# Cross-attention on one core: probability transposes issued two pairs further ahead, into four PSUM banks, in blocks of sixteen and eight

## What is computed

```python
q = _split_heads(hidden_states @ w_q, HEADS)
k = _split_heads(text @ w_k, HEADS)
v = _split_heads(text @ w_v, HEADS)
out_text = _sdpa(q, k, v)
...
k_ip = _split_heads(ip_h @ w_k_ip, HEADS)
v_ip = _split_heads(ip_h @ w_v_ip, HEADS)
out_ip = _merge_heads(_sdpa(q, k_ip, v_ip, mask=mask_ip))
out = out_text + IP_SCALE * out_ip
out = out @ w_out + b_out
out = out + residual
```

## Time and profile before

| what | value |
|---|---|
| median of 3 runs | 904.91 us (904.73 to 905.33) |
| the profiled execution's own time | 905.81 us |
| its span, first to last instruction | 904.0 us |
| PE busy | 882.5 us, 98% of the span |
| DVE, ACT, POOL busy | 726.6, 603.5, 540.0 us |
| mean granted TensorE clock | 0.992 of full speed |
| from group to group (start of scores to start of scores) | 50.4 to 50.5 us |

### The profile page before, as it was taken

One profiled execution on the slowest core, in us unless ns is written; L12 is line 12 of the kernel. 1 busy time (PEld: TensorE's weight loads), 2 busy tenths in 40 slices (PEclk: granted clock), 3 DMA queues, 4 the chain that ended last, 5 costly groups with the idle time before them and its releaser, 6 DMA issues.

```text
span 904.0 us, 13890 instructions
## 1 busy us (share of the span) xinstructions
PE 882.5 (98%) x4685; PEld 753.8 (83%) x4685; DVE 726.6 (80%) x1006; ACT 603.5 (67%) x986; POOL 540.0 (60%) x431
## 2 busy tenths in 40 slices
PE   7999999999999999999999999999999999999968
PEld 6889888888888888888888888888888888888846
DVE  6959579797888879797888879697888879797772
ACT  7556385876768485866767585867767584857550
POOL 5349669293755649293846648393847657392731
PEclk9999999999999999999999999999999999999978
DMA  9743322103030303003030303012030303010101
GB/s 318 271 162 117 96 69 86 44 1 131 1 124 1 131 0 102 21 13 118 0 123 0 131 0 122 2 33 98 0 123 0 131 0 116 0 59 1 47 12 59
DMA packets 34059, 64.63 MB, mean 71 GB/s; under 512 B 4464, under 2 KB 6512, under 8 KB 33904
## 3 DMA queue, kind: packets, MB, share of 16 engines
q1 hardware_dynamic: 33888, 62.97, 20.6%
q10 hardware_dynamic: 144, 1.31, 0.3%
HBM read 40.34 MB, written 23.59 MB: 71 GB/s over the span
## 4 chain that ended last, share of the span: by engine, by line
PE 82%; DVE 3%; ACT 1%; POOL 1%; issue 0%; DVEq 0%
PE bank L95 23%; PE bank L97 23%; PE bank L96 22%; PE bank L995 7%; PE bank L1004 4%; PE bank L1005 4%; DVE o_raw L905 1%; DVE pT_lo L898 1%; ACT oT_hi L820 0%; ACT pv_part L816 0%; POOL prob L185 0%; DVE total L226 0%; POOL prob L179 0%; DVE res L912 0%; ACT pT_hi L811 0%
## 5 line engine op out<-in xcount | busy, mean ns | idle before, releaser
L765 POOL TENSOR_TENSOR oT_lo<-o_raw,oT_hi 128x512 fp32r<-128x512 f32 x80 | 103.2, 1290 | 241.5 <-ACT oT_hi L820 241.5
L179 POOL TENSOR_TENSOR prob<-prob,top 128x1120 f32<-128x1120 f32 x126 | 178.8, 1448 | 0.0
L185 POOL TENSOR_TENSOR prob<-prob,inv 128x1120 f32<-128x1120 f32 x126 | 173.9, 1412 | 5.1 <-DVE inv L228 5.1
L95 PE MATMUL bank<-xT_hi,wq_hi 128*128 128x512 f32 x400 | 163.3, 408 | 0.0
L95 PE MATMUL bank<-oT_hi,wo_hi 128*128 128x512 f32 x400 | 156.7, 392 | 0.4 <-DVE res L912 0.4
L97 PE MATMUL bank<-xT_hi,wq_lo 128*128 128x512 f32 x400 | 156.8, 392 | 0.0
L96 PE MATMUL bank<-oT_lo,wo_hi 128*128 128x512 f32 x400 | 156.5, 391 | 0.0
L97 PE MATMUL bank<-oT_hi,wo_lo 128*128 128x512 f32 x400 | 156.5, 391 | 0.0
L96 PE MATMUL bank<-xT_lo,wq_hi 128*128 128x512 f32 x400 | 155.8, 389 | 0.0
L905 DVE TENSOR_TENSOR o_raw<-bank,pv_part 64x512 f32<-64x512 f32 x160 | 110.1, 688 | 47.2 <-ACT pv_part L816 44.8
L215 ACT ACTIVATE prob<-prob 128x1280 f32<-128x1280 f32 x64 | 81.6, 1277 | 78.6 <-POOL prob L179 78.5
(11 more groups left out here) (110 smaller groups left out, 1787.0 us busy)
## 6 DMA issues: line engine op xcount, KB each, us to landing
xin<-in_xT SPq DMA_DIRECT2D x16, 1280.0 KB, 6.8
outT<-res SPq DMA_DIRECT2D x80, 256.0 KB, 6.7
w_raw<-in_L_xattn_w_k SPq DMA_DIRECT2D x8, 320.0 KB, 5.6
w_raw<-in_L_xattn_w_k_ip SPq DMA_DIRECT2D x8, 320.0 KB, 5.7
w_raw<-in_L_xattn_w_v_ip SPq DMA_DIRECT2D x8, 320.0 KB, 3.1
w_raw<-in_L_xattn_w_v SPq DMA_DIRECT2D x8, 320.0 KB, 3.3
v_raw<-v_scratch SPq DMA_DIRECT2D x14, 140.0 KB
prob<-in_textT SPq DMA_DIRECT2D x8, 224.0 KB, 4.8
```

The source lines that it names most:

```text
L95: nc.tensor.matmul(dst, a_hi, b_hi, start=first, stop=False)
L179: ins = eng.tensor_tensor(s, s, top[:, t, n, :].unsqueeze(2).broadcast_to([P, HEADS, k1 - k0]), ALU.subtract)
L185: ins = eng.tensor_tensor(s, s, inv[:, t, n, :].unsqueeze(2).broadcast_to([P, HEADS, k1 - k0]), ALU.mult)
L765: nc.gpsimd.tensor_tensor(oT_lo[:, m, :], o_raw[:, m % 2, :], oT_hi[:, m, :].bitcast(F32), ALU.subtract).then_inc(oT_lo_done, 1)
```

## The change

- `t_bank` becomes banks 0 to 3 instead of 2 and 3, and pair p uses bank p % 4. The first four score units of a group now all wait for the last `pT_lo` of the group before.
- PE: the transposes of pairs 0 to 3 stand ahead of slot 0 (sixteen in a row). In slots 0, 1 and 2 the transposes of pairs 2s+4 and 2s+5 stand behind both pairs of the slot (eight in a row); slots 3 and 4 have none. Each waits for the `pT_lo` of pair p - 4.
- ACT and DVE: in each slot both `pT_part` now stand between the even and the odd move, or add. ACT's `pT_part(p)` gets a wait for `pv_ready` of pair p - 2, whose buffer of `pT_hi` it overwrites.

The buffers `pT_hi` and `pT_lo`, `v_bank`, and the waits of `pv_pair` stay as they are. No instruction that computes is added or removed.

```diff
-        s_bank, t_bank, v_bank = bank[0:4], bank[2:4], bank[4:6]
+        s_bank, t_bank, v_bank = bank[0:4], bank[0:4], bank[4:6]
...
         def score_unit(pe, g, n, b, new_batch):
-            if n < 2:
-                wait(pe, score_copied, UNITS * g)
-            elif n < 4:
+            if n < 4:
                 wait(pe, pT_lo_done, PAIRS * g)
...
                 def pT_part(g, p):
                     act.wait_ge(pT_ready, PAIRS * g + p + 1)
-                    nc.scalar.activation(pT_hi[:, p % 2, :], t_bank[p % 2][:], ACT.Copy).then_inc(pT_hi_done, 1)
+                    if p >= 2:
+                        act.wait_ge(pv_ready, PAIRS * g + p - 1)
+                    nc.scalar.activation(pT_hi[:, p % 2, :], t_bank[p % 4][:], ACT.Copy).then_inc(pT_hi_done, 1)
...
-                        for p in (2 * s, 2 * s + 1):
-                            move_pv(g, p)
-                            if p + 2 < PAIRS:
-                                pT_part(g, p + 2)
+                        move_pv(g, 2 * s)
+                        for p in (2 * s + 2, 2 * s + 3):
+                            if p < PAIRS:
+                                pT_part(g, p)
+                        move_pv(g, 2 * s + 1)
...
-                        for p in (2 * s, 2 * s + 1):
-                            add_pv(g, p)
-                            if p + 2 < PAIRS:
-                                pT_part(g, p + 2)
+                        add_pv(g, 2 * s)
+                        for p in (2 * s + 2, 2 * s + 3):
+                            if p < PAIRS:
+                                pT_part(g, p)
+                        add_pv(g, 2 * s + 1)
...
                 def p_transpose(g, p, shared):
-                    if p < 2:
+                    if p < 4:
                         pe.wait_ge(score_copied, UNITS * (g + 1))
                     else:
-                        pe.wait_ge(pT_lo_done, PAIRS * g + p - 1)
+                        pe.wait_ge(pT_lo_done, PAIRS * g + p - 3)
...
-                    p_transpose(g, 0, shared)
-                    p_transpose(g, 1, shared)
+                    for p in range(4):
+                        p_transpose(g, p, shared)
...
                         for p in (2 * s, 2 * s + 1):
                             pv_pair(g, p, b, new_batch)
-                            if p + 2 < PAIRS:
-                                p_transpose(g, p + 2, shared)
+                        for p in (2 * s + 4, 2 * s + 5):
+                            if p < PAIRS:
+                                p_transpose(g, p, shared)
```

More of the change, by code:

```diff
@@ L897, in pT_part @@
                     dve.wait_ge(pT_hi_done, PAIRS * g + p + 1)
-                    nc.vector.tensor_tensor(pT_lo[:, p % 2, :], t_bank[p % 2][:], pT_hi[:, p % 2, :].bitcast(F32), ALU.subtract).then_inc(pT_lo_done, 1)
+                    nc.vector.tensor_tensor(pT_lo[:, p % 2, :], t_bank[p % 4][:], pT_hi[:, p % 2, :].bitcast(F32), ALU.subtract).then_inc(pT_lo_done, 1)
                 def add_pv(g, p):
@@ L994, in p_transpose @@
                         src = prob[:, t * SW + p * P:t * SW + (p + 1) * P]
-                        ins = nc.tensor.transpose(t_bank[p % 2][:, t * P:(t + 1) * P], src, ident[:])
+                        ins = nc.tensor.transpose(t_bank[p % 4][:, t * P:(t + 1) * P], src, ident[:])
                     ins.then_inc(pT_ready, 1)
```

## The result

| | before | changed |
|---|---|---|
| median of 4 runs each | 904.84 us (904.73 to 905.33) | 939.79 us (938.98 to 939.95) |
| the profiled execution's own time, its span | 905.81, 904.0 us | 939.80, 938.0 us |
| start of scores to start of scores, groups 2 to 14 | 50.4 to 50.5 us | 52.4 to 52.7 us |
| first transpose to first score matmul, groups 2 to 14 | 19.35 to 19.51 us | 21.33 to 21.68 us |
| mean granted clock | 0.992 | 0.993 |

The changed kernel is slower by a factor of 1.0381 (95% interval 1.0367 to 1.0394), 35.0 us. The forecast was 937.2 us.

A forecast was written before the change was run, and what follows sets the result against it. PE, busy 98% of the span, bounds the kernel, with zero slack in ACT's and DVE's loop; 14 x 2.0 + 2.0 + 2.0 = +32 us gives 937.2 us on the median, range 926 to 952.

The forecast's parts named there:

- The even-move loop: ACT and DVE, one even move to the next: from 3.88 to 4.47 us with a q tile, 3.98 without.
- M0: End of slot 0's even move on ACT, forecast 5.05 us after the first transpose; M1 to M3 are slots 1 to 3.
- The waits on PE: PE in the values stage: pairs 5, 7, 8 and 9 wait 0.42, 0.15, 0.66 and 0.87 us.
- Group time: Each of the 16 groups, including 0 and 15, takes 2.0 us longer.
- Switches on PE: PE, fewer changes between transposes and matmuls: five joined runs save 0.02 to 0.03 us each, -0.1 us per group.
- pair 9's release: PE's last pair may start at M3 + 2.85 us, after slot 3's odd add on DVE; forecast 20.82 us.
- The far bound: PE, largest saving per switch between transposes and matmuls: 0.08 us each, -0.4 us per group.
- The bank sharing and the new waits: New waits of score units 0 and 1, the transposes and ACT's pv_ready: no cost.
- What ACT and DVE are late for next: Score copies and POOL's mask steps after the values stage: copies start 0.6 us later, costed at nothing.
- Rival 1: PE waits halve the clock when scores start: 1.7 us more in each of 16 groups, 964 us; chance 0.08.
- Rival 2: Faster: switches save 0.08 us each and ACT's and DVE's loop still fits PE's slot, 896 to 898 us; chance 0.04.
- rival 3: Nothing measurable: the lag stays below what PE notices, only 0.1 us per group saved, 903.3 us; chance 0.04.

The follow-up runs named there:

- Run 11: Changed kernel, groups 1 to 14 with tile rounded behind odd move and q steps 1, 3, 3, 3, 5, group 0 in old order: 902.65 us, ratio 0.9979.
- run 7: Kernel before with only the four transpose banks and their waits, every engine's order unchanged: 905.26 us, ratio 1.0003.
- run 4: Changed kernel with POOL making group 0's last residual ahead of the remainder of tile 3: 937.91 us, ratio 1.0367.
- run 2: Kernel before with only ACT's and DVE's new lists and the added pv_ready wait: 929.89 us, ratio 1.0278.
- run 1: Changed kernel with ACT's and DVE's old lists, keeping PE's new blocks and four banks: 917.68 us, ratio 1.0141.
- run 3: Changed kernel with ACT rounding the finished tile behind the odd move instead of ahead of the even move: 916.40 us, ratio 1.0128.
- run 5: Changed kernel with ACT's and DVE's old lists and q steps 2, 3, 3, 3, 4 instead of 3 each: 909.96 us, ratio 1.0049.
- run 8: Changed kernel with only the q steps per slot altered to 2, 3, 3, 3, 4: 930.18 us, ratio 1.0264.
- run 6: Changed kernel with tile rounded behind odd move, q steps 2, 3, 3, 3, 4, group 0's last residual earlier: 906.93 us, ratio 1.0019.

## Why the prediction was right, point by point

**The even-move loop.** Worked out 4.47 with a q tile and 3.98 without; measured 4.48 (M0 to M1), 3.99, 4.49. M0 to M3 were forecast at 5.05, 9.52, 13.50 and 17.97, and came at 5.04, 9.52, 13.51 and 18.00. Every duration in that sum came from rows of an engine that was already running back to back, and the change only put the same instructions in another order.

**The waits on PE.** Pairs 5, 8 and 9 start at 12.28, 19.43 and 20.83, forecast 12.37, 19.50 and 20.82; pair 7 at 16.35, as forecast. By the starts the four waits are 0.32, 0.11, 0.48 and 0.84, 1.75 together, where 2.1 was forecast. The difference does not reach the time: the stage ends 0.7 behind pair 9's start, and that start is set by its release. The releasers are those named: `o_raw` for pairs 5 and 9, `pT_lo` for pair 8. The row of pair 7 has no releaser, since its wait fits within the record of the matmul ahead.

**Group time.** Forecast +2.0, measured +2.04. Group 0: end of the stage forecast at 129.5, measured 129.55. Group 15: +2.0 within 1 us, measured 2.04 for everything from the start of its scores. That it came so close is in part luck: from the first transpose to the first output matmul it is 25.34 us instead of 22.91, 2.43 more, and 0.4 came back behind it, where the clock at the start of the output projection stands at half for 1.4 us instead of 3.4.

**Switches on PE, -0.1 per group.** In the changed kernel pair 9's release ends the stage, so that a saving on PE could not show there, and the prediction should not have counted it in the 2.0. Run 11 shows the term with the waits gone: the stage is 0.08 shorter where g is even and 0.2 where g is odd. Of the 0.2, about 0.12 is the later pair 0 that the odd groups had before, whose cause was not looked for. The far bound of 0.4 is ruled out.

**The bank sharing and the new waits at nothing.** Right by run 7.

**What ACT and DVE are late for next, at nothing.** This is the step that failed. It holds for groups 2 to 14. In group 1 it cost 1.4 us, since x has to be loaded behind POOL's residuals there and DVE's output add stands behind it (run 4). I had looked at score copies and mask steps alone, not at the DMA queue that POOL's end releases. The sum was 32; with this 1.4 it is 33.4, against 34.0, and 13 times 0.04 of the ordinary groups is most of the rest. (The medians differ by 35.0, since the profiled execution before the change was 1.0 above its median, and that of the changed kernel was not.)

**Mechanism.** The text put the loss on the loop that ACT's and DVE's lists lengthen. The runs show two costs of different kinds. The longer loop is about 1.3 us per group (run 2). The later start of the loop, 0.87 behind eight more transposes, is about 0.8 (run 1). Both stood in the sum, since pair 9's release was M0 + loops + 2.85; but I took M0's shift for something that the old slack would absorb, so my expectations for runs 1 and 3 were 14 and 12 us too low. The trace of before had the 0.11 us of slack on which this turns.

**Rival 1, the clock falls in every group.** Wrong. The granted clock is full from 9.8 to 893.9 us. In group 15 it falls, as it did before the change. Windows of the changed kernel: an ordinary group's stage, then group 15 (columns as in the earlier trace rows):

```profile
480.00:501.00 21.00, 19.86 (x105) 15.59 (x104) 13.74 (x21) 15.16 (x27) 5.14 (x4) 1.00 0.00 2
...
896.00:906.00 10.00, 8.06 (x38) 6.54 (x38) 5.35 (x10) 6.00 (x11) 1.27 (x1) 0.76 0.07 26
906.00:917.00 11.00, 7.86 (x22) 4.84 (x23) 6.75 (x12) 7.75 (x14) 3.47 (x3) 0.73 0.00 0
```

Four short waits in the stage leave the clock at 2.4 GHz (1.00). In group 15, where PE waits 4.48 us for POOL ahead of the transposes and then ahead of seven of the ten pairs, for up to 2.02 us, it falls to half for stretches. The Trainium skill ("TensorE: Matmul & The Clock Gate", section "A second HAM failure mode: psum-queue depth-cycling") tells of a bf16 kernel in which frequent short idles between groups of matmuls make the clock swing. The ordinary groups of this kernel do not show that: their waits are 0.11 to 0.84 us long and four in 21 us, and the granted clock stays at 1.00.

**Rivals 2 and 3.** Wrong as forecast: two slots of ACT and DVE take 8.47 us (13.51 - 5.04), not 7.74 or less, and pair 9's release does not come sooner. Run 11 shows what rival 3 would have looked like: it needs both the tile's rounding out of the way and a slot 0 that is shorter by what the transposes add.

## What to carry to other kernels

Where three engines hand one another small pieces in a loop, work out the loop's length on every engine and its slack against the engine that bounds, from starts in the timeline, before moving anything; a list that reads better on one engine (PE's blocks) can lengthen the loop on the others by placing a waiting instruction directly behind what it waits for. Work pulled ahead also delays the first hand-over by its own length, and a chain without slack carries that delay to its end: move as much filler work to the back as was pulled to the front (runs 5, 8 and 11). When a stage ends later, look at every queue that its last instructions release, DMA queues too, and at the first group as well as at the ordinary one.

## What the runs showed of the hardware that I had not expected

- A pair's first matmul that starts straight from a semaphore is followed by its second after 0.33 to 0.35 us instead of 0.23 (pair 9 of the changed kernel, 497.82 and 498.17), also where it had hardly to wait at all (run 6: 480.89 and 481.22, with no idle time listed). So in this kernel a pair that is released just in time already costs PE 0.1 us.
- Sixteen fp32 transposes in a row into four banks take 478.96 - 476.99 - 0.227 = 1.74 us, 0.109 each, the price that eight into two banks had in the earlier trace rows, although pair 0 stood 0.12 later in the groups with odd g before.
- Sharing two more banks between the scores and the transposes has no price that ten runs can show (run 7, 1.0003).
